# Layers' attention: one set of scores with queries on partitions, scaled probabilities turned by TensorE, in place of transposed scores and fp32 sums

## The reference

```python
def local_attention(q, k, v):          # b, h, n, d = 4, 8, 1024, 64
    bq, bk, bv = blocks of WINDOW = 128 tokens; bq * 8.0
    bk, bv = look_around(bk), look_around(bv)     # the block before and the own one
    sim = jnp.einsum('bhwid,bhwjd->bhwij', bq, bk)
    mask = (i < j) | (i > j + WINDOW) | (j == -1)
    attn = jax.nn.softmax(jnp.where(mask, -big, sim), axis=-1)
    return jnp.einsum('bhwij,bhwjd->bhwid', attn, bv)
for l in range(2):
    h = shift_token(x); q, k, v = split(h @ wqkv); q, k = rotary_xpos(l2norm(q) * qs, l2norm(k) * ks)
    x = x + local_attention(q, k, v) @ wo
    h = layernorm(shift_token(x)) @ w1 + b1; a, g = split(h, 2)
    x = x + (a * gelu(g)) @ w2 + b2
```

## Time and profile before

| | us |
|---|---|
| median of 3 runs (lowest, highest) | 2675.65 (2672.39, 2677.21) |
| the profiled execution, its own time | 2678.03 |
| its span, first to last instruction | 2676.1 |
| busy: PE, DVE, POOL, ACT | 2521.2, 1783.5, 1655.2, 1501.0 |
| stage `layers`, about | 70 to 1510 |

### The profile page before, as it was taken

How to read it: one execution, slowest core, us unless ns; L and a number is a source line. 1 busy time by engine, 2 the same in 40 slices (tenths; PEclk the granted TensorE clock), 3 DMA queues, 4 the chain that set the end, 5 groups by cost and what they waited for, 6 DMA issues and landing times. The chain is left out here.

```text
span 2676.1 us, 45404 instructions
## 1 busy us (share of the span) xinstructions
PE 2521.2 (94%) x17264; PEld 1729.0 (65%) x17264; DVE 1783.5 (67%) x3208; ACT 1501.0 (56%) x2039; POOL 1655.2 (62%) x1471
## 2 busy tenths in 40 slices
PE   5689999999999999999998599999999999999997
PEld 4577777777777777777776465655565556555553
DVE  5587777777877777777773187556756766666661
ACT  3257766777567766777665345344534544455443
POOL 2376666766766666666674246575657656665675
PEclk9799999999999999999999799999999999999998
DMA  7110000001111100000100100010101010100000
GB/s 265 53 35 11 31 29 29 29 19 38 45 33 34 39 29 29 29 13 29 33 21 17 64 9 9 1 32 1 33 1 32 1 32 1 32 1 25 1 25 8
DMA packets 68434, 79.93 MB, mean 30 GB/s; under 512 B 11048, under 2 KB 52348, under 8 KB 67196
## 3 DMA queue, kind: packets, MB, share of 16 engines
q1 hardware_dynamic: 68220, 77.03, 9.0%
HBM read 56.04 MB, written 20.97 MB: 29 GB/s over the span
## 5 line engine op out<-in xcount | busy, mean ns | idle before, releaser
L1648 ACT ACTIVATE g_pt<-ps 128x1024 f32<-128x1024 f32 x288 | 295.0, 1024 | 383.5 <-PE ps L1521 382.7
L1851 POOL TENSOR_TENSOR g_total<-g_total,g_pt 128x1024 f32<-128x1024 f32 x168 | 400.5, 2384 | 103.4 <-ACT g_pt L1648 95.5
L1756 DVE TENSOR_REDUCE g_most<-ps 128x2 f32<-128x1024 f32 (+3 forms) x256 | 262.6, 1026 | 98.3 <-PE ps L1492 93.3
L1533 PE MATMUL ps<-g_pt,g_latV 128*64 128x512 f32 x1152 | 307.8, 614 | 0.0
L1752 DVE TENSOR_TENSOR ps<-ps,g_mask 128x256 f32<-128x256 f32 x256 | 110.0, 430 | 140.9 <-PE ps L1492 139.6
L1213 POOL TENSOR_TENSOR l_act_lo<-l_u,l_act_hi 114x512 fp32r<-114x512 f32 x96 | 124.1, 1294 | 127.0 <-ACT l_act_hi L941 126.9
L1041 DVE CUSTOM_DVE_ANT_0 ps<-ps,l_mask 128x256 f32<-128x256 f32 (+1 forms) x512 | 190.8, 444 | 14.0 <-PE ps L677 13.2
L1848 POOL TENSOR_TENSOR g_total<-g_pt 128x1024 f32<-128x1024 f32 x56 | 133.5, 2384 | 97.1 <-PE ps L1544 54.5
L1099 DVE SCALAR_TENSOR_TENSOR l_u<-ps,l_b,l_u 114x512 f32<-114x512 f32 x96 | 70.6, 750 | 171.2 <-ACT l_u L931 139.0
L94 PE MATMUL ps<-l_h_hi,l_w_hi 128*114 128x512 f32 (+1 forms) x384 | 155.8, 406 | 16.9 <-POOL l_h_lo L1208 9.2
L94 PE MATMUL ps<-l_wqkv_hi,l_x_hi 128*128 128x512 f32 x384 | 164.0, 427 | 2.5 <-POOL l_x_lo L1142 1.8
(11 more groups left out here) (241 smaller groups left out, 7408.3 us busy)
## 6 DMA issues: line engine op xcount, KB each, us to landing
l_tab<-turns SPq DMA_DIRECT2D x64, 128.0 KB, 2.1
f_xtok<-in_L_attn_x_bld_dram SPq DMA_DIRECT2D x4, 1024.0 KB, 13.5
xnorm<-f_xT SPq DMA_DIRECT2D x4, 1024.0 KB, 4.6
l_xw<-xnorm SPq DMA_DIRECT2D x8, 512.0 KB, 4.3
mid<-l_xw SPq DMA_DIRECT2D x8, 512.0 KB, 3.5
l_xw<-mid SPq DMA_DIRECT2D x8, 512.0 KB, 4.3
state<-l_xw SPq DMA_DIRECT2D x8, 512.0 KB, 3.1
g_xn<-xnorm SPq DMA_DIRECT2D x8, 512.0 KB, 4.8
```

Of the source, the lines that this page charges most:

```text
L1533: last = pe.matmul(ps[64 * a:64 * a + 64, bank, :], latV[:, units[u][0] % 2, k, :], PT[:, i % NPT, a, :], start=(i == first[u]), stop=(i = ...
L1648: act.activation(PT[:, i % NPT, :, :], ps[:, bank:bank + 2, :], ACT.Exp).then_inc(s["ex"], 1)
L1756: dve.tensor_reduce(to, ps[:, bank:bank + 2, 0:n], AX_X, ALU.max, negate=True).then_inc(s["mx"], 1)
L1851: pool.tensor_tensor(to, to, here, ALU.add).then_inc(s["sum"], 1)
```

## The change

The second, transposed set of scores is dropped. The first one, with queries on partitions, is masked by DVE as before and read by ACT, which takes the exp with the maximum as its bias, one head at a time, and sums it in the same instruction (`l_sm`). DVE takes the reciprocals (`share`), POOL scales the probabilities `l_pp` by them (`scale`), PE transposes them (`flip`), ACT and DVE copy one half each to `l_pt` (`copy0`, `copy1`), `weigh` works as before, and its output is the context: ACT copies it to `l_ctx_hi`, DVE subtracts for `l_ctx_lo`. `peak`, `shifts`, `rows`, `step`, POOL's maskings, the sums, the guess and the Newton step go, and with them `l_shift`, `l_sel`, `l_r`, `l_total`, `l_ones` and their making in `stage_front`. `l_pp` has three buffers for half tiles (`NP`). The table of due times is another one throughout.

```diff
@@ class Flow @@
-        "pe": {"bias": (-27.37, 2, 4.02, 5.59), "proj": -2.57, "val": -2.41, "turn": -1.1, "scores": (-0.78, -0.73),
-               "shift": -0.48, "step": (0.76, 0.8), "weigh": 1.34, "total": 1.38, "wo": 5.17, "mean": 5.26,
...
+        "pe": {"bias": (-45.17, -4.73, 3.02, 4.57), "proj": -3.49, "val": -3.18, "turn": -2.04, "scores": (-1.8, -1.8),
+               "weigh": -0.03, "wo": 3.54, "mean": 4.01, "var": 4.41, "centre": 4.51,
...
+               "flip": (-0.84, -0.49)},
...
@@ PE @@
-                def shifts(g, bank):
...
-                def step(c, h, bank):
...
+                def flip(g, h, bank):
+
+                    pe.wait_ge(s["scaled"], 2 * g + h + 1)
+                    for a in range(2):
+                        for jj in range(2):
+                            for r in range(width(g) // P):
+                                last = pe.transpose(ps[:, bank + a, (2 * jj + r) * P:(2 * jj + r + 1) * P],
+                                                    PP[:, (2 * g + h) % NP, 2 * a + jj, r * P:(r + 1) * P], ident[:, :])
+                    last.then_inc(s["fl"], 1)
...
-                    pe.wait_ge(s["own"], 2 * (g + 1))
+                    for h in range(2):
+                        pe.wait_ge(s[f"pt{h}"], g + 1)
...
-                def totals(g, bank):
-                    pe.wait_ge(s["sum"], 2 * (g + 1))
-                    for a in range(2):
-                        last = pe.matmul(ps[64 * a:64 * a + 64, bank, :], ones64[:, :], total[:, a, :, :],
-                                         start=True, stop=True, skip_group_check=True)
-                    last.then_inc(s["ls"], 1)
...
@@ ACT @@
+                def exps(g, h, bank):
+
+                    i, n = 2 * g + h, width(g)
+                    if i >= NP:
+                        act.wait_ge(s["fl"], i - NP + 1)
+                    if g >= 2:
+                        act.wait_ge(s["rl"], i - 3)
+                    for a in range(2):
+                        for jj in range(2):
+                            at = 2 * a + jj
+                            act.wait_ge(s["mx"], 4 * i + 2 * a + 2)
+                            act.activation(PP[:, i % NP, at, 0:n], ps[:, bank + a, jj * 2 * P:jj * 2 * P + n], ACT.Exp,
+                                           bias=mx[:, g % 2, h, at:at + 1], scale=-1.0, accum_out=sm[:, g % 2, h, at:at + 1]
+                                           ).then_inc(s["ex"], 1)
+
+                def copy(g, bank):
+                    act.wait_ge(s["fl"], 2 * g + 1)
...
+                    act.activation(dst, src, ACT.Copy).then_inc(s["pt0"], 1)
...
-                    act.activation(dst, src, ACT.Relu, bias=1.0, scale=-1.0).then_inc(s["clip"], 1)
-                    act.wait_ge(s["clip"], i + 1)
-                    act.activation(dst, dst, ACT.Exp, bias=1.0, scale=-1.0).then_inc(s["ex"], 1)
...
@@ DVE @@
+                def share(g, h):
+                    i = 2 * g + h
+                    dve.wait_ge(s["ex"], 4 * (i + 1))
...
+                        dve.wait_ge(s["scaled"], i - 3)
+                    dve.reciprocal(rl[:, g % 2, h, :], sm[:, g % 2, h, :]).then_inc(s["rl"], 1)
+
+                def copy(g, bank):
+                    dve.wait_ge(s["fl"], 2 * g + 2)
...
+                    dve.tensor_copy(dst, src).then_inc(s["pt1"], 1)
+
+                def divide(g, bank):
+                    dve.wait_ge(s["chi"], g + 1)
+                    cols = slice(g % TC * P, (g % TC + 1) * P)
+                    dve.tensor_tensor(cl[:, :, cols], ps[:, bank, :].rearrange("p (j q) -> p j q", j=LP), ch[:, :, cols],
+                                      ALU.subtract).then_inc(s["clo"], 1)
...
@@ POOL @@
-                def add(c, h):
...
+                def scale(g, h):
+
+                    i, n = 2 * g + h, width(g)
+                    pool.wait_ge(s["rl"], i + 1)
+                    view = PP[:, i % NP, :, 0:n]
+                    pool.tensor_tensor(view, view, rl[:, g % 2, h, :].unsqueeze(2).to_broadcast([P, 4, n]), ALU.mult
+                                       ).then_inc(s["scaled"], 1)
```

More of the change, by code:

```diff
@@ L122, in stage_front @@
     Wq_hi, Wq_lo = wqkv
[L123 removed]
+    b1c, mask = small["b1"], small["mask"]
     H2, HD_, HALF = DH // 2, GH * DH, 3 * INNER // 2
@@ L392 @@
     PIECES, FIRST = 12, 4
-    TILES = ("load", "split", "proj", "norm", "val", "turn", "scores", "peak", "shift", "step", "weigh", "total", "divide")
+    TILES = ("load", "split", "proj", "norm", "val", "turn", "scores", "share", "scale", "flip", "copy0", "copy1", "weigh", "divide")
     DUE = {
         "sp": {
-               "bring": (-50.02, -27.03, -12.94, -10.67, -6.28, -3.66, 2.52, 3.58, -11.97, -7.69, -6.39, -4.62, -3.9, -2.75, -0.65, 0.4, 1.25, 1.95, 2.54, 4.22),
-               "load": -6.38, "xload": 1.56, "store": 5.04},
-        "pe": {"bias": (-27.37, 2, 4.02, 5.59), "proj": -2.57, "val": -2.41, "turn": -1.1, "scores": (-0.78, -0.73),
-               "shift": -0.48, "step": (0.76, 0.8), "weigh": 1.34, "total": 1.38, "wo": 5.17, "mean": 5.26,
[L400 to L404, removed]
-        "dve": {
[L406 to L411, removed]
-    }
@@ L413 @@
[L413 to L416, removed]
+               "bring": (-148.89, -109.09, -95.31, -68.59, -67.32, -53.46, -19.53, -14.79, -35.39, -23.75, -20.72, -20.72, -19.38, -16.46, -15.17, -15.14, -14.49, -12.6, -12.4, -11.87),
@@ L418, in __init__ @@
+    BANKS = {"proj": (2, "dve", "proj"), "val": (1, "act", "val"), "turn": (2, "dve", "turn"), "scores": (2, "act", "scores"),
+             "flip": (2, None, None), "weigh": (1, "dve", "divide"), "wo": (2, "dve", "wo"), "mean": (1, "dve", "mean"),
+             "var": (1, "act", "var"), "centre": (1, "dve", "centre"), "up": (2, "dve", "up"), "down": (2, "dve", "out"),
+             "bias": (1, "dve", "bias")}
     def __init__(self):
@@ L459, in place @@
             now = self.due("pe", e)
-            until = self.due(engine, (reader,) + (e[1:2] if e[0] == "down" else e[1:]))
+            if e[0] == "flip":
+                until = self.due(("act", "dve")[e[2]], (f"copy{e[2]}", e[1]))
+            else:
+                until = self.due(engine, (reader,) + (e[1:2] if e[0] == "down" else e[1:]))
             if n == 2:
@@ L953, in _ @@
                         turn(e[1], flow.bank[e])
-                    elif e[0] == "shift":
-                        rows(e[1], flow.bank[e])
-                    elif e[0] == "step":
+                    elif e[0] == "scores":
                         exps(e[1], e[2], flow.bank[e])
-                    elif e[0] == "total":
-                        guess(e[1], flow.bank[e])
+                    elif e[0] == "copy0":
+                        copy(e[1], flow.bank["flip", e[1], 0])
                     elif e[0] == "divide":
-                        divide(e[1])
+                        divide(e[1], flow.bank["weigh", e[1]])
                     elif e[0] == "mean":
```

209 lines of the change are left out of this document (66 added, 143 removed).

## The result

The changed kernel takes **2557.16 us** (median of 4 runs, 2555.01 to 2560.24) against 2674.6 for the kernel before beside it (4 runs, 2672.39 to 2677.21): a ratio of 0.9561, 95% interval 0.9545 to 0.9578, so 117.4 us or 4.4% less. The forecast was 2570 (2535 to 2625), that is 105.6 less than the 2675.65 it started from. The profiled execution took 2560.24 us and its span is 2558.5, against 2676.1 before: 117.6 less.

A forecast was written before the change was run, and what follows sets the result against it. PE (TensorE) was taken as the bound: 2678.0 profiled - 117.8 net PE work - 4 edges + 16.7 new waits = 2572.9; the median of runs is 2.4 lower, so 2570 us, range 2535 to 2625.

The forecast's parts named there:

- rival 1: Layers stage: new chain has slack everywhere, two thirds of PE's 38.5 us idle go; 2535 to 2545 us, chance 0.15.
- `step` 134.4, `totals` 60.8: PE time saved over 64 tiles: second, transposed scores 2.10 us each, fp32 sums 0.95 us each.
- The shift 28.2: PE, turned row of shifts gone: 0.44 us a tile, 28.2 in all, mostly the wait for DVE's `l_shift`.
- Flips 105.6: PE, new transposes of scaled probabilities: 120 eights at 0.88 us add 105.6 us; bounds 95 and 133.
- The other engines cost nothing under PE's tile: DVE, ACT and POOL changes cost nothing while each stays under PE's new tile of about 19.2 us.
- New waits, +16.7: PE hand-overs at `flip` and `weigh`: charged once at what the wait for `l_shift` costs now, 16.7 us.
- Edges -4: Behind the last tile: PE's 5.62 us wait for `l_ctx_lo` gets about 4 us shorter (0 to 5).
- The first tiles: nothing: Start of the layers stage: no change in time expected at the first tiles.
- What would show it: Signs in the new profile: tile pace, PE busy share, flip starts, waits at `flip`, other engines below 80%.
- My bounds: DVE's two new reciprocals of four numbers a tile: nothing, or 1.19 us as the cast behind POOL.

The follow-up runs named there:

- the doublings: Issued twice: `step` matmuls in the kernel before, 2782.3 us; `totals` matmuls in the kernel before, 2702.03 us; `flip` transposes in the kernel after, 2639.73 us.
- the other kernel: The kernel after, with DVE's subtraction in `divide` made three times instead of once: 2617.36 us, +58.1 against the kernel after.

## Why the prediction was right, and where not

The direction was right, and so was the main mechanism: PE is the bound, and the second scores and the sums cost it more than the flips. The time came out 12.8 us under the forecast, inside the range, and as near to rival 1, whose upper end was 2545 (12.2 away). That it is so near is luck in part. By blocks the touched steps gave 18.0 us less than forecast and the first scores came 11.9 late, while the waits charged, 16.7, did not come and the untouched blocks and edges gave 25.5 more than the 4 forecast. By its steps:

- **`step` 134.4, `totals` 60.8.** 135.6 and 67.8 us by blocks. As block sizes right; as prices of the path they were too high, since doubling them cost 106 and 26.
- **The shift 28.2.** 3.4 and 19.9 of wait, 23.3 together. But taking the wait alone gives 6.3: most of such a wait turns up elsewhere unless the tile as a whole gets lighter.
- **Flips 105.6.** 117.8 by blocks, and `weigh`, taken as the same, 9.1 more. The eights themselves cost 0.84 to 0.88, as predicted; 49 of the 128 blocks have the scores behind them; the 41 of them with eight transposes take 0.96 from start to start or more, and there a wait for `l_qk_lo` is counted in. With these three steps the touched blocks gave 99.8 us, not 117.8.
- **The other engines cost nothing under PE's tile.** This is the step that failed, though the sum hides it. Their loads came out at or below the forecast (DVE 13.2 us a tile where I had 13.4 to 15.8, ACT 12.5 where I had at most 14, POOL 11.8 where I had less than 14.2). Yet lighter engines under an unchanged PE gave 24 us before the change, and 1.4 us a tile put back on DVE cost 58 after it. Ahead of PE's blocks there are short waits, once in a tile or in four, that no share of busy time shows.
- **New waits, +16.7.** Not paid. `flip` waits once; the order gives its chain the room that I had counted. The unchanged blocks took 29.5 us less instead. Rival 1, *the new chain has slack everywhere*, was nearer on waits: it had two thirds of PE's 38.5 us of idle time go, and half went (1160 - 1140.62 = 19.4 are left).
- **Edges -4.** Behind the last tile the wait fell from 5.62 to 1.51 us, 4.1 less, as said; the whole stretch behind the last scores fell by 15.4, of which I can place only these 4.1. "The first tiles: nothing" was wrong by +11.9 at the first scores and by -8.4 at the 9th tile.
- **What would show it.** Tiles 19 to 19.5 us apart: 19.15. PE at 95% or more: 98.3. Eights in 0.8 to 1.0 us: 0.79, and 0.96 ahead of the scores. Waits at `flip` under 20 us: 2.0. Others below 80%: 69. All met, within 0.01, and it is a warning that they were: these signs fit a kernel in which the prices that I gave account for only half of the gain, as the doublings have it.

**What stays open.** The price that doubling showed for each part would give -106 - 26 - 6 + 80 = -58 us. Lighter engines in the kernel before give another -24. Some 35 us are left, or up to 6 more, since that run too has the wait for `l_shift` shorter, and so holds part of the 6. They are either those parts' interplay (prices for adding work need not hold for taking it away) or the new order of the shared work; the new work in the old order was not tried, since in each order that I found for it the engines wait for one another in a ring. It is unsettled.

## What to carry to other kernels

Where a loop of fixed order is 97% busy on one engine, price a change by the starts of its blocks, and expect an eighth to a half of the work that is added to be taken in by other blocks (12%, 20% and 52% in the three doublings), unless the other engines change with it. An engine at 69% of its time can still be the one that is waited for: look for the place where the bound engine already waits 0.3 us, once in a tile or once in a group, and ask what each new instruction does there. A start that is late by 12 us may cost 6 or nothing by the tenth tile.

## What the runs showed of the hardware that I had not expected

- **A wait of 1.7 us mostly cost 3.4, and once 5.** Behind the 1.74 us wait above, the clock was at its 1.2 GHz level for 7 us, 3.4 us lost; behind ten more at the same place 1.7 us were lost each time. It is not the wait alone: of two waits of 1.37 us at that place one was followed by such a fall and one was not, and in the kernel before, the longest wait for `l_shift` left the clock where it was, as its timeline and windows show:

```profile
358.10 0.30 PE L682 MATMUL ps<-ident,l_shift 128*128 128x128 f32 x1 [1.69 <-DVE l_shift L1054]
```
```profile
356.00:358.00 2.00, 0.41 (x2) 0.00 (x0) 2.00 (x3) 0.00 (x0) 1.91 (x1) 1.00 0.82 260
358.00:360.00 2.00, 1.90 (x11) 1.39 (x13) 1.93 (x4) 1.36 (x3) 0.00 (x0) 1.00 0.02 7
360.00:362.00 2.00, 2.00 (x34) 1.86 (x33) 1.97 (x3) 1.96 (x3) 0.97 (x1) 1.00 0.00 0
```

  There, projections of 512 columns stand on both sides; in the other kernel scores of 128 or 256 columns follow the wait. Whether that is the reason was not tried.
- **The clock also fell without any wait.** In the two windows of the kernel after shown with the result, PE is busy all of 584 to 588 us and the clock goes from 1.00 to 0.58; what PE did just before are scores and then the 16 matmuls of one column of `var` (583.73 to 585.50). Between 200 and 1300 us the kernel after loses 13.6 us to the clock, the one before 1.7. It is not how full PE is that does it: with the flips doubled PE is idle for 4.4 us there in place of 13.6, and 5.1 are lost. What sets it is not shown.
- **The reciprocal does not stand behind POOL as the cast and the subtraction of eight numbers did.** It takes 171 ns on average in 128 times, where the cast took 1193 and the subtraction 1025. By the trace, 53 of the 64 casts ran beside a POOL instruction and took 1.40 us on average, the 11 others 0.17; 55 of the 128 reciprocals ran beside one and took 0.17, as the others did. My bounds had been nothing and 1.19; the Trainium skill's reading (page SBUF — State Buffer, SBUF: two separate sides), by which it need not wait, agrees.
- **An exp with a sum is two instructions on ACT**, 484 and 216 ns by their durations; on the timeline two of 128 columns, with the read between them, start 0.34 us apart, two of 256 columns 0.45.
